# Attention and expert kernel: masks of the row maxima on TensorE, and another order of routing, scatters and GpSimd work

## What is computed

```python
scores = einsum('bhtd,bhsd->bhts', q, k) * scale
scores = where(causal, -inf, scores)            # softmax over s, times v: seq_out
M_all = cumsum(outer(Jw, Jw) * decay_inv) * decay_fwd
mem_score = (1 - alpha) * sum(rd_M * rd) + alpha * sum(rd_M * rd_M)
x = layernorm(x + (seq_out + gated * mem_val) @ out_w.T + out_b)
topk_vals, topk_idx = top_k(x @ wr + br, 2)     # 4 experts, 2 chosen
x = layernorm(x + sum of the two gated experts)
```

## Time and profile before

| | |
|---|---|
| three runs | 1140.71, 1144.14, 1146.69 us; median 1144.14 |
| the profiled execution | 1146.64 us, its span on the trace 1144.9 us |
| TensorE | busy 968.0 us, 85% of the span, 8044 matmuls |
| VectorE | busy 828.7 us, 72%, 2944 instructions |
| ScalarE | busy 492.3 us, 43% |
| GpSimd | busy 427.8 us, 37%, 374 instructions |
| transfers | 85.29 MB, mean 74 GB/s |
| mean granted clock of TensorE | 0.93 |

### The profile page before, as it was taken

The page is one execution under the profiler, slowest core; times in us unless marked ns, Lnnn a source line. Parts: engine busy times, 40 slices in busy tenths (PEclk is TensorE's granted clock), DMA queues, the critical chain, the costliest instruction groups (busy, mean ns, idle before and its releaser), DMA issues.

```text
span 1144.9 us, 28049 instructions
## 1 busy us (share of the span) xinstructions
PE 968.0 (85%) x8044; PEld 698.7 (61%) x8045; DVE 828.7 (72%) x2944; ACT 492.3 (43%) x1047; POOL 427.8 (37%) x374
## 2 busy tenths in 40 slices
PE   3689998797897897988879874999999999999940
PEld 1244656455454554555555553898989989999830
DVE  3647789497596795895965786777777777777737
ACT  4045464463462553644526552433333343333314
POOL 8206245265074262352743723122323323223231
PEclk8689999899898998998989886999999999999975
DMA  5742103303213213023015022123323323233347
GB/s 163 171 137 63 51 20 92 78 19 118 55 47 100 61 64 106 1 86 83 20 61 236 31 100 74 30 48 46 53 49 46 51 43 54 46 46 52 50 88 242
DMA packets 70121, 85.29 MB, mean 74 GB/s; under 512 B 18504, under 2 KB 61000, under 8 KB 69000
## 3 DMA queue, kind: packets, MB, share of 16 engines
q1 hardware_dynamic: 55728, 62.29, 18.8%
q0 software_dynamic: 14304, 21.90, 10.3%
HBM read 48.13 MB, written 35.91 MB: 73 GB/s over the span
## 4 chain that ended last, share of the span: by engine, by line
PE 64%; DVE 11%; issue 7%; DMA 5%; ACT 5%; SPq 4%; POOL 2%; another core or an unknown queue 1%; DVEq 0%; ACTq 0%; POOLq 0%
PE st L1239 8%; PE sm L1239 8%; PE sm L1250 8%; PE pv L1250 8%; PE ms L1020 6%; PE st L1060 5%; PE pv L1080 5%; PE sm L1101 3%; PE ms L999 3%; PE ms L1156 2%; PE st L1062 2%; PE ms L1128 2%; PE ms L1227 1%; DMA arena_a<-max_row 1%; PE ms L1130 1%
## 5 line engine op out<-in xcount | busy, mean ns | idle before, releaser
L913 ACT ACTIVATE arena_b<-st 128x512 f32<-128x512 f32 x320 | 188.7, 601 | 233.3 <-PE st L1062 192.4
L1464 DVE CUSTOM_DVE_ANT_0 junk<-sm,mask_ts 128x512 bf16<-128x512 f32 (+3 forms) x512 | 222.1, 486 | 55.5 <-PE sm L1101 51.5
L803 POOL DMA_INDIRECT sums<-arena_b x70 | 111.1, 1587 | 291.2 <-DVE arena_b L1720 253.3
L1060 PE MATMUL st<-arena_a 128*128 128x384 f16 (+3 forms) x512 | 137.8, 313 | 45.2 <-issue 31.0
L1101 PE MATMUL sm<-arena_a 128*128 128x512 f16 (+3 forms) x512 | 119.6, 309 | 35.3 <-DVE maxes L1464 21.9
L1700 DVE TENSOR_TENSOR arena_b<-arena_b 128x256 f16<-128x256 f32 x280 | 119.7, 427 | 9.6
L1060 PEld LDWEIGHTS st<-arena_a 128*128 128x128 f16 x512 | 51.3, 100 | 121.2 <-issue 70.7
L1698 DVE CAST arena_b<-arena_b 128x256 f16<-128x256 f32 x280 | 87.5, 312 | 41.5 <-ACT arena_b L974 39.3
L1239 PE MATMUL st<-arena_b,arena_a 128*128 128x256 f16 x840 | 115.5, 275 | 1.8 <-DVE arena_b L1674 1.8
L1250 PE MATMUL pv<-arena_a,arena_b 128*128 x864 | 116.7, 273 | 0.0
L974 ACT ACTIVATE arena_b<-st,arena_b 128x256 f32<-128x256 f32 x140 | 66.3, 474 | 116.8 <-PE st L1239 106.0
(11 more groups left out here) (246 smaller groups left out, 1685.4 us busy)
## 6 DMA issues: line engine op xcount, KB each, us to landing
arena_b<-slots SPq DMA_DIRECT2D x37, 260.0 KB
arena_a<-w SPq DMA_DIRECT2D x5, 1024.0 KB, 8.4
arena_b<-x_tr SPq DMA_DIRECT2D x8, 512.0 KB, 3.6
q_rows<-arena_b SPq DMA_DIRECT2D x32, 128.0 KB
k_rows<-arena_b SPq DMA_DIRECT2D x32, 128.0 KB
arena_a<-q_rows SPq DMA_DIRECT2D x32, 128.0 KB
arena_a<-k_rows SPq DMA_DIRECT2D x32, 128.0 KB
res<-x_tok POOLq DMA_DIRECT2D x8, 512.0 KB, 5.4
```

Of the source, the lines that this page charges most:

```text
L803: pool.indirect_dma_start(sums, bass.IndirectOffsetOnAxis(ap=token_now[:, 1 - par, m:m + 1], axis=0), y_out[1 - par][:, m, :], None, compu ...
L913: act.activation(probs[:, q, :], st_ps[piece % 2][:, :], ACT.Exp, scale=SCORE_SCALE).then_inc(exp_done, 1)
L1060: pe.matmul(out[:, at:at + width], ks[:, h % 2, h // 2, s * P:(s + 1) * P], qs[:, h // 2, s * P:T], start=m == 0, stop=False, skip_group_c ...
L1464: last = dve.tensor_tensor_reduce(junk[:, piece % 3, at:at + width], sm_ps[piece % 3][:, at:at + width], mask_ts[:, T - width:T], 1.0, NEG ...
```

## The change

1. **Maxima.** TensorE adds the mask to the maxima blocks as it does for the scores, with the roles of mask and identity changed. Two blocks whose last 128 columns carry a mask get it in one matmul of 256 columns over a strided output; pieces 0 and 1 have one block and a matmul of 128. VectorE then takes plain maxima over the whole bank, one `tensor_reduce` a piece, four results of 128 columns each, into `maxes_of_blocks`. In the stage `maxima_rows` four small reductions join these to `maxes`; the transposes wait for them (`maxes_done`). `mask_ts` and `junk` are gone.
2. **Scores.** The second block's mask goes with the first's, in one matmul of 256 columns.
3. **Routing.** The stages from `normalise` to `rank` stand earlier in the list.
4. **GpSimd** follows the list: minors, outer products, both biases (each in four parts) and the eight scatters are stages of their own. The order in its queue is: minors 0 and 1, the low part of x, minors 2 to 8, outer products, value biases, scatters 0 to 4, row bias 0, scatter 5, row bias 1, scatter 6, row bias 2, scatter 7, row bias 3.
5. **The residual load** is issued by SP at the end of its step. The scatters count on one semaphore per parity.

```diff
@@ stages_of_a_step @@
-        5: [("queries", 3), ("weights", 11), ("weights", 12), ("nothing", 1)],
-        6: [("first_weights", 0), ("normalise", 0), ("normalise", 1), ("normalise", 2), ("x1_rows", 0), ("x1_rows", 1), ("first_weights", 1), ("normalise", 3)],
-        7: [("x1_rows", 2), ("x1_rows", 3), ("first_weights", 2), ("weights", 13)],
-        8: [("logits", 0), ("memory", 0), ("memory", 1), ("first_weights", 3)],
-        9: [("gates", 0), ("rank", 0), ("weights", 14), ("weights", 15), ("nothing", 2), ("nothing", 3), ("memory", 2), ("memory", 3)],
+        5: [("normalise", 0), ("queries", 3), ("normalise", 1), ("normalise", 2), ("x1_rows", 0), ("normalise", 3), ("x1_rows", 1), ("weights", 11), ("weights", 12), ("nothing", 1)],
+        6: [("first_weights", 0), ("x1_rows", 2), ("x1_rows", 3), ("first_weights", 1), ("logits", 0)],
+        7: [("first_weights", 2), ("gates", 0), ("weights", 13)],
+        8: [("rank", 0), ("memory", 0), ("memory", 1), ("first_weights", 3)],
+        9: [("weights", 14), ("weights", 15), ("nothing", 2), ("nothing", 3), ("memory", 2), ("memory", 3)],
...
+    after(("lines_in", 3), ("exterior", 0), ("exterior", 1))
+    for n in range(2, 9):
+        after(("scores", 8 + n), ("exterior", n))
+    after(("scores", 17), ("own", 0))
+    for n in range(1, 9):
+        after(("scores", 18 + n), ("own", n))
+    for n in range(C):
+        after(("scores", 27 + n), ("value_bias", n))
+        after(("scores", 36 + n), ("row_bias", n))
+    for n in range(2 * C):
+        after(("scores", 32 + n), ("scatter", n))
@@ SP's step, at its end @@
+                if ab:
+                    if t:
+                        sp.wait_ge(x1_out_s, n_of(16 * (i - 1)))
+                        sp.wait_ge(x1t_ready, n_of(4 * (i - 1)))
+                        sp.wait_ge(scattered[par], n_of(128 * half(i)))
+                        n_of.stand(i)
+                    load_residual(i, par)
@@ GpSimd's step @@
-                    pool.tensor_tensor(res[:, :, 0:D], res[:, :, 0:D], out_b[:, :].unsqueeze(1).broadcast_to([P, C, D]), ALU.add).then_inc(res_done, 1)
...
-                    for k in range(2):
-                        for n in range(C):
-                            pool.indirect_dma_start(slots, bass.IndirectOffsetOnAxis(ap=slot_i[:, par, k, n:n + 1], axis=0),
-                                                    res[:, n, :], None).then_inc(scattered, 16)
+                def row_bias(n):
...
+                    pool.tensor_tensor(res[:, n, 0:D], res[:, n, 0:D], out_b[:, :], ALU.add).then_inc(res_done, 1)
+
+                def scatter(n):
+                    if n == 0:
+                        pool.wait_ge(routed, n_of(i - 1))
+                        n_of.stand(i)
+                    pool.indirect_dma_start(slots, bass.IndirectOffsetOnAxis(ap=slot_i[:, par, n // C, n % C:n % C + 1], axis=0),
+                                            res_of[par][:, n % C, :], None).then_inc(scattered[par], 16)
@@ TensorE, scores @@
-                        last = pe.matmul(out[:, at:at + P], ident_b[:, :], mask_st[:, :], start=False, stop=True, skip_group_check=True)
-                    last.then_inc(st_ready, 1)
+                    if q < 4:
+                        pe.matmul(out[:, 0:P], ident_b[:, :], mask_st[:, :], start=False, stop=True, skip_group_check=True).then_inc(st_ready, 1)
+                    else:
+                        both = out[:, :].rearrange("p (m t) -> p m t", t=P)[:, 0:4:3 if q < 8 else 2, :]
+                        pe.matmul(both, ident_b[:, :], mask_st[:, :].unsqueeze(1).broadcast_to([P, 2, P]),
+                                  start=False, stop=True, skip_group_check=True).then_inc(st_ready, 1)
@@ TensorE, maxima @@
+                    if piece % 5 < 2:
+                        pe.matmul(out[:, 3 * P:4 * P], mask_st[:, :], ident_b[:, :], start=False, stop=True, skip_group_check=True).then_inc(sm_ready, 1)
+                    else:
+                        both = out[:, 2 * P:4 * P].rearrange("p (m s) -> p m s", m=2) if piece % 5 < 4 else \
+                            out[:, :].rearrange("p (m n s) -> p m n s", m=2, n=2)[:, :, 1, :]
+                        pe.matmul(both, mask_st[:, :], ident_b[:, :].unsqueeze(1).broadcast_to([P, 2, P]),
+                                  start=False, stop=True, skip_group_check=True).then_inc(sm_ready, 1)
@@ TensorE, maxima to rows @@
-                    pe.wait_ge(sm_read, n_of(40 * i + 40))
+                    pe.wait_ge(maxes_done, n_of(4 * i + 4))
@@ VectorE, maxima @@
-                        last = dve.tensor_tensor_reduce(junk[:, piece % 3, at:at + width], sm_ps[piece % 3][:, at:at + width], mask_ts[:, T - width:T],
-                                                        1.0, NEG, ALU.add, ALU.max, maxes[:, col:col + 1])
-                    last.then_inc(sm_read, 1)
+                    dve.tensor_reduce(maxes_of_blocks[:, piece // 5, piece % 5, :], sm_ps[piece % 3][:, :].rearrange("p (m s) -> p m s", s=P),
+                                      AX.X, ALU.max).then_inc(sm_read, 1)
+
+                def maxima_of_rows(_):
...
+                    dve.tensor_reduce(by_tile[:, :, :, 3], by_piece[:, 0:2, :, :], AX.X, ALU.max).then_inc(maxes_done, 1)
+                    dve.tensor_reduce(by_tile[:, :, :, 2], by_piece[:, 2:4, :, 0:3], AX.X, ALU.max).then_inc(maxes_done, 1)
+                    dve.tensor_reduce(by_tile[:, :, :, 1], halves, AX.X, ALU.max).then_inc(maxes_done, 1)
+                    dve.tensor_reduce(by_tile[:, :, :, 0], by_piece[:, 2:4, :, 3:4], AX.X, ALU.max).then_inc(maxes_done, 1)
```

More of the change, by code:

```diff
@@ L83, in stages_of_a_step, with after @@
         order.insert(order.index(("maxima", h + 22)) + 1, ("flip", h))
+    def after(stage, *more):
+        at = order.index(stage) + 1
+        order[at:at] = more
+    after(("lines_in", 3), ("exterior", 0), ("exterior", 1))
[9 more added lines that the diff above has]
+        after(("scores", 32 + n), ("scatter", n))
     return order
@@ L256, in attention_and_ffn @@
         mask_st = sb("mask_st", [P, P], BF16)
-        mask_ts = sb("mask_ts", [P, T], F32)
         before = sb("before", [P, P], BF16)
@@ L399, in run @@
                 parts[stage] = t
+            parts["scatter"] = t
             parts["memory_scores"], parts["last_memory_scores"] = t and at != B + 1, at == B
@@ L594, in _ @@
             schedule(sp, step)
-            sp.wait_ge(scattered, 128 * B)
+            for done in scattered:
+                sp.wait_ge(done, 64 * B)
             sp.wait_ge(fill_out, 16 * (E + 1))
@@ L790, in _ @@
             later_constants()
-            for n in range(2):
-                load_residual(n, n)
             schedule(pool, step)
```

171 lines of the change are left out of this document (86 added, 85 removed).

## The result

The changed kernel takes **1167.5 us** (median of four runs, 1161.1 to 1169.9) beside 1142.4 us of the kernel before (four runs, 1140.4 to 1146.7): ratio 1.0205, 95% interval 1.0161 to 1.0249, 25 us slower. The forecast was 1130, its range reached to 1168. The profiled execution of the changed kernel is the fastest of them (1161.07 us, span 1159.2), so beside the profiled execution of the kernel before (1146.64 us) its rows show 14 us of the loss and not 25.

A forecast was written before the change was run, and what follows sets the result against it. TensorE and VectorE were taken to bound the attention part, with TensorE stalling at step ends beside scatters. Terms -40 + 18 + 9 - 3 = -16 us from 1146.6 gave 1130.6, in the median 1128, stated as 1130 us; range 1110 to 1168.

The forecast's parts named there:

- +24 for the rest: All terms outside the step ends: masks 18, longer chain of small reductions 9, last step -3 us.
- the stall travels: Rival, chance 0.32: TensorE's stall moves with the scatter burst into mid-step, 8.3 us per burst; about 1166 us.
- What moves with the routing: Normalising, x1 transposes and logits pass some 4 to 9 maxima pieces each; ScalarE has room, no cost in the forecast.
- If the tails become like the quiet one: Step ends, transposes of maxima to next scores: earlier scatters make six like the scatter-free first; -40 us (-25 to -50).
- Excess of 50.0: Six later step ends total 76.00 us, 50.0 us above six times the scatter-free first one's 4.33 us.
- Masks +18: Maxima masks moved to TensorE: 28 us more matmuls, half of 19.9 us waits returned; net +18 us (+8 to +28).
- Chain +9: Step end: transposes wait for four small VectorE reductions, TensorE stands 1.35 us seven times; +9 us (0 to +14).
- Last step -3: Last step, TensorE waiting 11.84 us for scattered rows: routing passes three weight conversions less; -3 us.
- The reductions at 0.60 us: VectorE's plain maxima over 512 elements: 0.60 us each, 192 us in all, against 222.1 us with mask.
- The routing meets POOL's outer products: Rival, chance 0.12: expert choice on VectorE waits out POOL's outer products, 3 us more in six steps; 1148 us.
- the sign that I had named: A comparison step of the routing on VectorE above 1.2 us beside POOL would show the outer-products rival.
- Half the stall stays: Rival, chance 0.11: longer scatter burst still reaches into the step end; gain there 25 instead of 40, 1145 us.

## Why the prediction was wrong

The direction was wrong and the forecast 37 us too low. I had -40 for the tails and +24 for the rest; the runs have about -17 for the stall and +42 for the rest. So two steps failed, with about the same weight. One is the first rival's (the stall travels), the other no rival had. Step by step:

- **"What moves with the routing: normalising, the transposes of x1 and the logits ... ScalarE ... has room for it; at most the transposes wait once a step for the fourth query block, which I leave to the range"** is the first step that failed; it put the moved work at nothing. The place was right and the price was left out: it is 11.6 us of waits in the list, more with the lower clock behind them. The choice of experts, moved along, cost another 15.9 us of waits, since it now fell where VectorE's maxima were wanted at once. I asked whether the engines had time for the moved work, and not who stands directly behind it in each queue. The routing alone cost 17 us on a chip that has no stall; with places chosen by the waits it gains 8.
- **"If the tails become like the quiet one ... they return 50.0 less 6 x 1.7 us: -40 us"** is the second. The tails gave 49, but the scatters stall TensorE in the middles too: 22 us came back there, and more in step 8. What was saved of the stall is 21 us in the six steps (467 - 423 = 43 before, 479 - 457 = 22 after) and 17 in whole runs. Even the bound of -25 was too hopeful.
- **"Excess of 50.0"**: the stall in these tails was 43. I took the 4.45 us at the turn of the loop, 290.89 to 295.35 in the tail of step 3 (15.26 us, the longest of the six), for stall; on a quiet chip 3.97 of it stays.
- **Masks +18**: inside its bounds once the rest is in place, where they cost 11 us (quiet) and 8 (stalling). The parts, 28 us of matmuls less 10 of waits, measure 19.1 and 8.5 us in six steps, which by an estimate is 25 and 11 over eight batches; 2.7 us of tails were in no term. Alone, with the chain, masks cost 10 us where I had 27: the extra matmuls partly filled TensorE's pauses, and its clock in the middles of the masks' kernel is 1.00 in five of six, where the kernel before on a quiet chip has 0.95 to 0.97 in four of six. Inside the changed kernel the maxima's matmuls cost 12 to 17.
- **Chain +9**: 8.1 us of waits, and gone with the small reductions placed early, on a quiet chip at least.
- **Last step -3**: it was +5.6 in steps 8 and 9, and +3.4 on a quiet chip (114.9 against 111.5). The slots pass no conversion at all: in both traces the same eight stand ahead of them in step 9 (VectorE, from 673.43 and from 685.75 on). The last of these (stage 13) now stands between the choice and the slots.
- **The reductions at 0.60 us**: 0.61.
- **The stall travels** (0.32): it does, at half its size or somewhat more, some 4 us a burst instead of 7 (22 and 43 us over six), where the rival had all of it. Beyond that its sum rested on "masks +18, chain +9" and not on the waits of the routing; that it ended at 1166 is partly luck.
- **The routing meets POOL's outer products** (0.12): in four of the six steps it met the value bias instead, and three comparisons took 0.7 us each beside pieces of 0.73 us on POOL. In steps 2 and 7 it met an outer product first, and the sign that I had named, a comparison above 1.2 us, is there in step 7: 1.38 us from 577.35 on, beside POOL's 1.46 us from 577.25 on. TensorE's waits behind the choice are the longest in these two steps, 3.3 and 3.6 us against 2.2 to 2.3. But the choice takes 4.1 to 5.5 us, before 5.0 to 5.3, and over the six steps 27.0 against 30.7, so this rival is out as the main cause. The Trainium skill's rule ("SBUF — State Buffer", section "Who interferes with whom"), that a VectorE instruction with two SBUF inputs contends with a GpSimd one that reads SBUF, agrees with these rows: with the bias in quarters, VectorE is held 0.7 us at a time and no longer 2.38, and 1.38 us beside an outer product.
- **Half the stall stays** (0.11): about that much stays, though in the middle and not in the tail, and its time of 1145 was too low by the waits of the routing.

What adds up on a quiet chip: routing alone 17, masks alone 10, both 42. The remaining 15 is an interaction. The masks use up TensorE's pauses, the routing's new waits then have nothing to hide in and push the clock down. This is argued from the busy time and the clock above; no run separates the two. Nor does a run show which of the places matters most: taken singly, two of them gave 6 us and next to nothing, and all of them together 40 (1105.2 against 1144.7).

## What to carry to other kernels

A stage moved ahead in one order for all queues is costed by what stands right behind it on each engine. A block of 4 us of small operations can hold up an engine whose results another engine takes every 0.6 us, and a transpose placed one stage before its input is done costs its wait and a stretch at the lower clock. A wait taken away singly may only turn up elsewhere, as with the transposes here; the gain came when all of them went. Before a stall is counted as a gain, look whether it is there in every run's conditions, and where it will be if its cause only moves. The gain over the kernel before, 8 us on a quiet chip and 35 on a stalling one, lay in the order of the stages; the masks' move, made to relieve VectorE, gained in none of the pairs measured.

## What the runs showed of the hardware

- One kernel has two times, 1102 to 1105 and 1142 to 1148 us, each steady within a group of runs. Nearly all of the difference is one thing: 43 us in the six tails beside the scatters. The scatters themselves have about the same spacing in both (1.27 and 1.29 us each), and the expert part takes 388.8 us in both, from its first matmul (670.63 and 711.24 us) to the end of its last (1059.43 and 1100.06).
- On the stalling kind TensorE's releases reach ScalarE late while scatters are under way, also in the middle of a step (an exponential at 279.55 for scores whose last matmul started at 276.18). The lateness follows the burst when it is moved. In the step without maxima it doesn't show in the kernel before (111.2 and 111.9 us to the expert part, quiet 111.5), but it does in the changed one (116.8 and 119.5, quiet 114.9). What makes it, and why it came out at 22, 13 and 43 us for three orders of the same scatters, stays open. That the scatters cause it is argued from their place alone: kernels without scatters, and scatters spaced out on a stalling chip, weren't measured.
- Short waits of TensorE were followed by matmuls at the lower clock level (0.61 instead of 0.38 us, after waits of 0.56 and 1.34 us). With 20.6 us of waits taken out of six steps, the same matmuls cost 12.1 us less busy time.
